# Column sums of 15 adjacency tiles: matmuls with a picking matrix, or adds on VectorE and one matmul pair a tile

## The reference

```python
# layer 0
adj_hat = adj + eye(8192)
d = 1 / sqrt(sum(adj_hat, axis=1))            # needs every row sum of adj
x1 = layernorm(x + relu((adj_hat * d[:, None] * d[None, :]) @ (x @ W0) + b))
# layer 1
s = x1 @ W1
out = layernorm(x1 + pair_norm(relu(s + adj @ s + x1 @ Wself)))
```

## Time and profile before

| | |
|---|---|
| time, median of 3 runs (lowest to highest) | 1904.98 us (1902.94 to 1906.03) |
| profiled execution: its own time; span | 1904.95 us; 1903.1 us |
| TensorE busy | 1732.4 us, 91% of the span |
| VectorE busy | 1454.5 us, 76% |
| ScalarE busy | 1209.3 us, 64% |
| the summing matmuls L964 | 4 x 224 instructions |
| mean granted TensorE clock | 0.961 of full speed |

### The profile page before, as it was taken

The page is one execution under the profiler, slowest core; times in us unless marked ns, Lnnn a source line. Parts: engine busy times, 40 slices in busy tenths (PEclk is TensorE's granted clock), DMA queues, the critical chain, the costliest instruction groups (busy, mean ns, idle before and its releaser), DMA issues.

```text
span 1903.1 us, 20444 instructions
## 1 busy us (share of the span) xinstructions
PE 1732.4 (91%) x7682; PEld 1407.5 (74%) x7682; DVE 1454.5 (76%) x1898; ACT 1209.3 (64%) x1644; POOL 21.5 (1%) x34
## 2 busy tenths in 40 slices
PE   1099999999999999978999999999989999999983
PEld 0077778888887888767787788788868888877862
DVE  4486687686878679975777575575589999999987
ACT  3576686676856646654554554454468888888865
POOL 0000000000000000100000000000000000000001
PEclk7599999999999999999999999999999999999995
DMA  9999999999899568753444545545579999999943
GB/s 399 421 421 420 421 371 421 420 364 416 332 399 370 217 274 352 273 183 123 164 174 169 184 162 196 184 170 199 194 298 393 386 387 386 386 368 374 386 174 88
DMA packets 80291, 572.02 MB, mean 301 GB/s; under 512 B 8961, under 2 KB 8961, under 8 KB 12097
## 3 DMA queue, kind: packets, MB, share of 16 engines
q1 hardware_dynamic: 76608, 557.88, 74.9%
q0 software_dynamic: 3584, 12.85, 2.2%
HBM read 566.49 MB, written 4.19 MB: 300 GB/s over the span
## 4 chain that ended last, share of the span: by engine, by line
PE 75%; DVE 11%; DMA 9%; ACT 3%; issue 1%; SPq 0%; POOL 0%; ACTq 0%; DVEq 0%
PE acc L982 18%; PE acc L984 18%; PE acc L988 18%; DVE lo L687 6%; DMA s<-in_adjN 4%; PE pD L964 4%; PE pC L964 4%; DMA zr<-in_adjT 2%; DMA raw<-in_adjT 2%; ACT hi L514 1%; PE pA L982 1%; PE pA L984 1%; PE pA L988 1%; PE pB L982 1%; PE pB L988 1%
## 5 line engine op out<-in xcount | busy, mean ns | idle before, releaser
L982 PE MATMUL acc<-hi,rhi 128*128 128x512 f32 x1792 | 719.0, 401 | 44.3 <-DVE lo L687 26.5
L984 PE MATMUL acc<-lo,rhi 128*128 128x512 f32 x1792 | 702.1, 392 | 0.0
L687 DVE TENSOR_TENSOR lo<-raw,hi 128x1024 fp32r<-128x1024 f32 x528 | 627.4, 1220 | 77.1 <-ACT hi L514 73.1
L514 ACT ACTIVATE hi<-raw 128x1024 fp32r<-128x1024 f32 x528 | 544.3, 1055 | 168.5 <-PE pD L964 78.9
L988 PE MATMUL acc<-hi,rlo 128*128 128x512 f32 x1792 | 556.2, 392 | 0.0
L982 PEld LDWEIGHTS acc<-hi,rhi 128*128 128x128 f32 x1792 | 338.9, 189 | 135.3 <-DVE lo L687 42.6
L984 PEld LDWEIGHTS acc<-lo,rhi 128*128 128x128 f32 x1792 | 338.8, 189 | 73.1 <-issue 5.0
L988 PEld LDWEIGHTS acc<-hi,rlo 128*128 128x128 f32 x1792 | 338.5, 189 | 72.3
L687 DVE TENSOR_TENSOR lo<-zr,hi 128x1024 fp32r<-128x1024 f32 x188 | 225.3, 1222 | 43.6 <-ACT hi L514 40.7
L514 ACT ACTIVATE hi<-zr 128x1024 fp32r<-128x1024 f32 x188 | 197.2, 1059 | 53.5 <-PE acc L988 16.9
L686 DVE TENSOR_TENSOR rlo<-zr,rhi 128x256 fp32r<-128x256 f32 x123 | 52.1, 423 | 176.7 <-ACT hi L514 176.6
(11 more groups left out here) (164 smaller groups left out, 1526.8 us busy)
## 6 DMA issues: line engine op xcount, KB each, us to landing
raw<-in_adjT SPq DMA_DIRECT2D x264, 1024.0 KB, 5.5
zr<-in_adjT SPq DMA_DIRECT2D x94, 1024.0 KB, 6.2
raw<-in_adjN SPq DMA_DIRECT2D x54, 1024.0 KB, 17.6
o<-in_adjT SPq DMA_DIRECT2D x32, 1024.0 KB, 10.5
s<-in_adjN SPq DMA_DIRECT2D x30, 1024.0 KB, 18.9
s<-in_adjT SPq DMA_DIRECT2D x30, 1024.0 KB, 14.7
zr<-in_adjN SPq DMA_DIRECT2D x28, 1024.0 KB, 19.5
s<-in_xT POOLq DMA_DIRECT2D x8, 512.0 KB, 8.0
```

Source lines behind the costliest of these rows:

```text
L514: S.activation(hi[n % DEEP][:, :], slice_of(chunk, j), ACT.Copy).then_inc(hi_ready, 1)
L687: V.tensor_sub(lo[n % DEEP][:, :], slice_of(chunk, j), hi[n % DEEP][:, :].bitcast(f32)).then_inc(slice_split, 1)
L982: T.matmul(banks[h][:, :], a, hi[n % DEEP][:, part], start=opens, stop=False, skip_group_check=True)
L984: T.matmul(banks[h][:, :], a, lo[n % DEEP][:, part], start=False, stop=False, skip_group_check=True)
```

## The change

Of the 28 tiles left of the diagonal, 15 are no longer summed by `add_sums`: in stages 2 to 6 every tile but the first, that is five, four, three, two and one of them. Each of these gets a number (`folded`). VectorE adds the tile's eight raw slices into one 128 x 1024 tile `fold` (`fold_in`, seven adds: one with the first chunk, two with each other, each behind that chunk's two `lo`). When TensorE has multiplied the first chunk of the next tile, it sums `fold` over the partitions with two float32 matmuls (`add_fold`) into the same banks. There is one `fold`, so the first add of a tile waits until `add_fold` of the tile before has read it. A folded chunk's buffer comes free with its last add instead of its last `lo`. In stages 2 to 6 the fourth chunk of each tile right of the diagonal, which VectorE reduced (L693, 15 of them), is summed by ScalarE.

```diff
--- before.py
+++ after.py
@@ -17,6 +17,7 @@
     cached: bool = False
     act: bool = False
     summed: bool = False
+    folded: int = -1
     stage: int = -1
     tail: int = -1
     buf: str = ""
@@ -91,13 +92,14 @@
         return len(visits) - 1
 
     TAIL = 2 * Q
+    folds = 0
     products = []
     beside = defaultdict(list)
     for k in range(NB):
         sums = []
         for c in range(k + 1, NB):
             for q in range(Q):
-                sums.append(Chunk("sum", k, c, q, act=(q % 2 == 0 if k == 0 else q != 3), stage=k))
+                sums.append(Chunk("sum", k, c, q, act=(q % 2 == 0 if k == 0 else q != 3 or k > 1), stage=k))
         kept = [Chunk("keep", k, k, q, stage=k) for q in range(Q)]
         if k == 0:
             chunks += kept + sums
@@ -106,8 +108,10 @@
         multiply_block(products, k - 1, k - 1, (L0,), new_visit(k - 1, (L0,), 1, first=(k == 1)),
                        cached=True, stage=k)
         for i in range(k, NB):
+            fold = k > 1 and i > k
             multiply_block(products, i, k - 1, (L0,), new_visit(i, (L0,), 1, first=(k == 1)),
-                           summed=True, stage=k)
+                           summed=not fold, folded=folds if fold else -1, stage=k)
+            folds += fold
         for i, c in EXTRA.get(k, ()):
             multiply_block(products, i, c, (L0,), new_visit(i, (L0,), 1), stage=k)
         for n in range(first, len(products)):
@@ -169,12 +173,19 @@
     after_row0 = next(c for c in chunks if c.stage == 1)
 
 
+    FOLD = Q * JB - 1
+
+    def fold_steps(q):
+
+        return (q + 1) * JB - 1
+
+
     slices = act_sums = dve_sums = 0
     for chunk in chunks:
         if chunk.kind == "mul":
             chunk.base = slices
             slices += JB
-            chunk.freed = ("split", slices)
+            chunk.freed = ("split", slices) if chunk.folded < 0 else ("fold", FOLD * chunk.folded + fold_steps(chunk.q))
             visits[chunk.visit].end = slices
         elif chunk.kind == "sum" and chunk.act:
             act_sums += 1
@@ -329,6 +340,7 @@
 
         xT_blk = s1[:, 0:BLK]
         colsum = s1[:, BLK:2 * BLK]
+        fold = s1[:, 7 * BLK:8 * BLK]
         rsum = [s1[:, 2 * BLK + r * NB * BG:2 * BLK + (r + 1) * NB * BG] for r in range(2)]
         kept = o1
         raw = {f"raw{r}": raw_own[r][:, :] for r in range(4)}
@@ -364,6 +376,8 @@
         act_summed = sem("act_summed")
         dve_summed = sem("dve_summed")
         col_step = sem("col_step")
+        fold_step = sem("fold_step")
+        fold_summed = sem("fold_summed")
         sums_closed = sem("sums_closed")
         sums_read = sem("sums_read")
         deg_turned = sem("deg_turned")
@@ -408,7 +422,7 @@
         dve_normed = sem("dve_normed")
         out_done = sem("out_done")
 
-        raw_free = {"split": slice_split, "act": act_summed, "dve": dve_summed}
+        raw_free = {"split": slice_split, "act": act_summed, "dve": dve_summed, "fold": fold_step}
         bank_free = {"row": row_summed, "l0": l0_read, "dual": dual_read, "added": dual_added, "l1": l1_read,
                      "x1": x1_ready, "s1": s1_ready, "self": self_added}
 
@@ -465,6 +479,7 @@
             for b in ("s34", "s56"):
                 by, count = phase1_last[b]
                 pool.wait_ge(raw_free[by], count)
+            pool.wait_ge(fold_summed, folds)
             for k in FINAL_ROWS:
                 pool.dma_start(groups(s1[:, k * BLK:(k + 1) * BLK]),
                                x[k * BLK:(k + 1) * BLK, :].rearrange("(g p) f -> p g f", p=P)).then_inc(x_in[k], 16)
@@ -686,6 +701,20 @@
                                 V.tensor_sub(rlo[s][:, :], (zr, s1)[l][:, at:at + JB * P], rhi[s][:, :].bitcast(f32))
                     V.tensor_sub(lo[n % DEEP][:, :], slice_of(chunk, j),
                                  hi[n % DEEP][:, :].bitcast(f32)).then_inc(slice_split, 1)
+                if chunk.folded >= 0:
+                    fold_in(chunk)
+
+            def fold_in(chunk):
+
+                at = FOLD * chunk.folded + fold_steps(chunk.q) - JB
+                if chunk.q == 0:
+                    if chunk.folded > 0:
+                        dve.wait_ge(fold_summed, chunk.folded)
+                    V.tensor_add(fold, slice_of(chunk, 0), slice_of(chunk, 1)).then_inc(fold_step, 1)
+                    return
+                for j in range(JB):
+                    dve.wait_ge(fold_step, at + j)
+                    V.tensor_add(fold, fold, slice_of(chunk, j)).then_inc(fold_step, 1)
 
             def sum_rows(chunk):
                 dve.wait_ge(*landed(chunk))
@@ -991,6 +1020,16 @@
                         last = add_sums(chunk, n)
                     last.then_inc(slice_multiplied, 1)
 
+            def add_fold(chunk):
+
+                pe.wait_ge(sums_read, closed[0])
+                pe.wait_ge(fold_step, FOLD * (chunk.folded + 1))
+                to = pick[:, NB - 1 - chunk.row:NB - 1 - chunk.row + P].bitcast(f32)
+                for h in range(H):
+                    last = T.matmul(sums[h][:, :], to, fold[:, h * HALF:(h + 1) * HALF],
+                                    start=False, stop=False, skip_group_check=True)
+                last.then_inc(fold_summed, 1)
+
             def close_sums(k):
                 pe.wait_ge(col_step, (k + 1) * (JB * Q - 1))
                 to = pick[:, NB - 1 - k:NB - 1 - k + P].bitcast(f32)
@@ -1069,6 +1108,9 @@
             first_product(0)
             for n, chunk in enumerate(mul_chunks):
                 multiply(chunk)
+                over = mul_chunks[n - 1]
+                if n > 0 and over.folded >= 0 and over.q == Q - 1:
+                    add_fold(over)
                 after_rows(n)
                 if chunk.stage > 0 and chunk.tail == 0:
                     close_sums(chunk.stage)
```

## The result

The changed kernel takes 1960.63 us (median of 4 runs, 1959.36 to 1963.88) against 1904.72: a ratio of 1.0298, 95% interval 1.0283 to 1.0314. 1950 with a range of 1925 to 1991 was forecast. The span of the profiled execution went from 1903.1 to 1957.6 us, +54.5.

What follows compares the result with a forecast made beforehand. TensorE was taken to bound stages 2 to 6, VectorE after folding; stage changes of +18.7, +15.4, +11.4, -1.7 and +1.6 made +45 us on 1904.95: 1950 us, own range 1935 to 1965, widened to 1925 to 1991.

Steps and rivals of the forecast that it cites:

- The pace: Folded tiles in stages 2 to 6: VectorE's 18.6 us a tile replaces TensorE's 18.2, so nothing of 84 us is gained.
- The kept adds: VectorE's seven colsum adds for the diagonal tile, 8.3 us a stage, uncovered in stages 2 to 4.
- a lead: VectorE enters each folded stretch ahead of TensorE: 3.5 us, net 2 us saved a stage in stages 2 to 4.
- the rival of no change: Stages 2 to 6: VectorE's unseen head start covers diagonal-tile adds (25) and half the add_fold waits (18): 1907 us; chance 0.03.
- ScalarE's extra sums: 15 row reduces moved from VectorE in stages 2 to 6: 31 us, costed at nothing since ScalarE idles 156.
- the later release of buffers: Folded chunks' buffers come free some 2.4 us later; costed at nothing, sign of error ScalarE waiting for a DMA.
- The sum: Stages 2 to 6 added up as 146.4, 124.3, 102.2, 74.2 and 70.7 us: together +45 us.
- the ten waits: VectorE's first add of later folded tiles in a stage waits for the previous tile's add_fold: 3.5 us each, at least 3.3.
- the clock rival: TensorE falls to half clock in the folded stretch; each add_fold wait grows to 7.6 us, +41, 1991 us; chance 0.10.
- The faster rival: Stages 2 to 6: VectorE stays over 3.5 us ahead at each folded tile's end, no waits: 1891 us; chance 0.07.

Runs made afterwards that it cites:

- The first experiment: Against the changed kernel, TensorE's add_fold of a tile moved ahead of the next tile's first chunk instead of behind it: 1917.14 us, 1.006 of the kernel before.

## Why the prediction was right

**The pace.** 18.6 us of VectorE a folded tile were worked out and 18.59 measured, once the wait was out of the way. That this replaces TensorE's 18.2 is shown twice: by the reduces, of whose 34 us on VectorE some 22 come back beyond the longer waits, and by the six missing adds.

**The kept adds** in stages 2 to 4 were to lie bare at 8.3 us each. Six of the seven narrowed to 8 columns gave 18.8 us in three stages, where 18 was worked out. So they were not covered by a lead, as the rival of no change had it.

**ScalarE's extra sums and the later release of buffers** were costed at nothing. The first is shown: nothing without folding (0.9995), and with it the kernel gets slower when ScalarE is relieved (1991.25). The second was not tried by itself. Its sign was to be ScalarE waiting for a load, and that became rarer: `hi` waited 23.1 us for loads from `in_adjT` in 15 waits between 240 and 711 us before, and 16.5 us in 7 between 240 and 770 in the changed kernel.

**The sum.** Take the ten waits out of it, and the forecast for the five windows is 132.4, 113.8, 95.2, 70.7 and 70.7 us. The first experiment has the waits out of the kernel; its windows:

```profile
238.39:369.10 130.71, 111.57 (x445) 84.04 (x444) 116.41 (x116) 99.17 (x139) 0.53 (x1) 0.95 0.94 379
369.10:483.50 114.40, 95.88 (x374) 71.90 (x373) 107.11 (x109) 84.36 (x120) 0.53 (x1) 0.93 0.94 372
483.50:578.65 95.15, 79.14 (x321) 60.26 (x320) 88.35 (x92) 67.63 (x96) 0.53 (x1) 0.95 0.88 348
578.65:651.76 73.11, 64.30 (x270) 49.12 (x269) 69.82 (x75) 51.82 (x72) 0.53 (x1) 0.95 0.85 338
651.76:721.66 69.90, 62.83 (x270) 48.79 (x269) 69.39 (x75) 42.45 (x52) 0.53 (x1) 0.98 0.72 293
```

Together 483.3 against 482.8. The single stages are off by -1.7 to +2.4 us and these cancel, so the half microsecond is in part luck; the lead of 2 us a stage was not measured by itself.

**The waits: the term that was mis-sized.** 3.5 us each was taken; the ten last 41.3 us, and the kernel without them is 43.5 us faster, so 4.35 each. That is 8.5 us of the 10.6 between 1950 and 1960.63, and lies within the 3.3 to 5 us that gave the narrower range, 1935 to 1965. Eight of the ten last 3.67 to 3.74: the lower bound of 3.3 and 0.4, where 0.2 was taken for hand-overs. In the wait shown above 0.2 of these lie between the end of `add_fold` (some 336.9) and VectorE's add (337.12); 0.17 lie in TensorE's two slices, which take 2.89 us behind an idle time (332.31 to 335.20), where 2.72 was taken. Two last 5.31 and 6.31, and these are the clock rival's. The longer one, in VectorE's and TensorE's timelines and in windows of TensorE's clock (length, busy, clock, DMA share, GB/s):

```profile
582.85 2.47 DVE L736 TENSOR_TENSOR s<-s,o 128x1024 f32<-128x1024 f32 x2
585.24 2.35 DVE L702 TENSOR_TENSOR lo<-s,hi 128x1024 fp32r<-128x1024 f32 x2
593.90 1.23 DVE L713 TENSOR_TENSOR s<-s 128x1024 f32<-128x1024 f32 x1 [6.31 <-PE pD L1029]
```

```profile
586.51 0.79 PE L1011 MATMUL acc<-hi,rhi 128*128 128x512 f32 x1 [4.04 <-DVE lo L702]
...
591.79 1.21 PE L1029 MATMUL pC<-s,pick 128*128 128x512 f32 x2
```

```profile
584.00:588.00 4.00, 1.49 (x4) 0.67 1.02 424
588.00:592.00 4.00, 4.00 (x11) 0.50 0.24 98
```

Ahead of the next tile two folding adds (580.45) and then two kept adds (582.85) stand together on VectorE, so TensorE idles 4.04 us, comes back at half clock (0.67 and 0.50), and takes the two slices and the beginning of `add_fold` at half speed, while VectorE stands 6.31 us.

**The clock rival** was thus right about the clock and wrong about the price. TensorE ran at 0.89 to 0.96 of full speed in these windows; that lengthened two waits, by 1.6 and 2.6 us, and not ten by 4. Elsewhere VectorE was late anyway: the first experiment, at 0.93 to 0.98, comes out at the sum above, which has no term for the clock. Where TensorE sets the pace half clock does cost, as in the run with two chunks folded. The rule of the Trainium skill that small idle times between groups of matmuls make the clock swing (TensorE: Matmul & The Clock Gate, section "A second HAM failure mode: psum-queue depth-cycling") is borne out by this trace as to the swing, 0.50 here against 1.00 throughout in the earlier trace rows, but not for every small idle time (last section).

**The faster rival** needed VectorE to be ahead of TensorE at each tile's end. No run made it so with seven adds in each of 15 tiles and the kept adds whole (1917.14 at best; 1898.36 with most of the kept adds left out). Twelve tiles folded whole, and better five slices of eight folded, did turn the sign, which the prediction did not consider: it weighed the change as it stood.

## What to carry to other kernels

Before work is moved from the engine that binds, add up what each engine then has to do in one tile and one chunk of that very stretch: here TensorE's 18.2 us became VectorE's 18.6, although VectorE had idled for a fifth of the time. A balance must hold within the depth of the buffers between the engines (here four slices, of which VectorE's lead is two); a mean over a tile promised 1885 to 1897 and gave 1907, while about as much folding, spread evenly, gave 1888. And when one engine hands a shared buffer back to another, look at what stands ahead of the hand-back in program order: one call moved ahead of another was worth 43.5 us, and the wait came back as soon as the work ahead of the call grew (three chunks folded).

## What the runs showed of the hardware

How long TensorE idles does not decide by itself whether the clock falls. In the changed kernel an idle time of 2.45 us was followed by matmuls 0.43 us apart (339.53, above), one of 2.83 us in front of 367.80 by matmuls at full clock. TensorE's timeline there, and the window behind it (length, busy, clock, DMA share, GB/s):

```profile
367.80 0.50 PE L1011 MATMUL acc<-hi,rhi 128*128 128x512 f32 x1 [2.83 <-DVE lo L702]
```

```profile
368.00:372.00 4.00, 4.00 (x25) 1.00 0.38 162
```

Between 324 and 336 us and between 344 and 356, where TensorE idled 1.25 to 1.66 us behind each chunk, the granted clock stayed at 1.00. In the five windows of the changed kernel every fall of the clock stood behind an idle time of 2.20 us (in front of 390.53) or more, but not every such idle time brought one.
